# Graph network of three hops on one core: five chunks of ten groups, and four edits around them

## The reference

```python
agg = h; out = 0; rel = edge_emb[edge_type]
for _ in range(3):
    left  = agg[head] @ q_w
    right = tanh((rel * agg[tail]) @ k_w)
    att   = sum(left * right, axis=1)
    w     = softmax of att over the edges of one head
    summed = segment_sum(w[:, None] * rel * agg[tail], head)
    agg   = summed / max(cnt, 1)
    agg   = agg / max(norm(agg), 1e-12)
    out   = out + agg + h
return x + out
```

## Time and profile before

| | us |
|---|---|
| median of 3 runs (lowest, highest) | 2566.2 (2558.34, 2572.57) |
| the profiled execution | 2568.1 |
| its span | 2566.3 |
| PE busy (matmuls) | 1126.9, 44% |
| DVE busy | 1454.0, 57% |
| ACT busy | 858.7, 33% |
| POOL busy | 1190.2, 46% |

### The profile page before, as it was taken

One profiled execution on the slowest core, in us unless ns is written; L12 is line 12 of the kernel. 1 busy time (PEld: TensorE's weight loads), 2 busy tenths in 40 slices (PEclk: granted clock), 3 DMA queues, 4 the chain that ended last, 5 costly groups with the idle time before them and its releaser, 6 DMA issues. The chain is left out here.

```text
span 2566.3 us, 24723 instructions
## 1 busy us (share of the span) xinstructions
PE 1126.9 (44%) x5196; PEld 897.6 (35%) x5196; DVE 1454.0 (57%) x7228; ACT 858.7 (33%) x2657; POOL 1190.2 (46%) x1219
## 2 busy tenths in 40 slices
PE   0112333355454545553100257688734667655430
PEld 0011222244344324453100135467623455454320
DVE  8863664453364545544339657667654644657664
ACT  3312442332333423333126433344433232222320
POOL 1034434454545354466650255552035554647666
PEclk9999655555565655556555577788567777765555
DMA  5532322221222222322225464453144644636654
GB/s 203 207 139 88 129 93 67 68 80 57 71 67 68 71 71 70 115 80 92 77 81 213 172 189 146 132 150 109 63 153 139 189 127 115 174 85 168 168 142 130
DMA packets 192463, 305.35 MB, mean 119 GB/s; under 512 B 31210, under 2 KB 113458, under 8 KB 183686
## 3 DMA queue, kind: packets, MB, share of 16 engines
q1 hardware_dynamic: 153914, 230.79, 26.9%
q0 software_dynamic: 38400, 72.99, 10.8%
HBM read 176.41 MB, written 132.67 MB: 120 GB/s over the span
## 5 line engine op out<-in xcount | busy, mean ns | idle before, releaser
L646 POOL DMA_INDIRECT tr<-in_x_dram,tidx x200 | 191.4, 957 | 508.4 <-DMA acc_d<-xr 297.1
L1574 PE MATMUL ps<-rt,wr 128*125 128x128 f32 x1200 | 266.3, 392 | 245.1 <-issue 85.0
L1503 PE MATMUL ps<-ident,rt 128*128 128x128 f32 x600 | 144.6, 385 | 449.2 <-DVE rt L1169 206.8
L646 POOL DMA_INDIRECT tr<-agg_d,tidx x200 | 191.9, 959 | 288.4 <-DMA agg_d<-rt 138.4
L1574 PEld LDWEIGHTS ps<-rt,wr 128*125 128x125 f32 x1200 | 233.0, 288 | 263.4 <-DVE wr L1094 145.5
L1381 ACT ACTIVATE sqj<-ps,invc 125x128 bf16<-125x128 f32 x600 | 212.3, 373 | 328.5 <-remote 161.1
L646 POOL DMA_INDIRECT tr<-ntab_d,tidx x200 | 193.7, 969 | 260.9 <-DVE rt L1169 196.3
L1341 ACT COPY turns<-ps 128x512 f32<-128x512 f32 x150 | 87.8, 585 | 617.1 <-PE ps L1503 351.1
L1503 PEld LDWEIGHTS ps<-ident,rt 128*128 128x128 f32 x600 | 98.0, 196 | 482.0 <-issue 248.4
L1094 DVE TENSOR_SCALAR wr<-segbc,lcol,wcol 128x125 f32<-128x125 uint8 x600 | 177.9, 349 | 153.7 <-remote 111.4
L658 POOL DMA_INDIRECT ntab_d<-rt,lidx x200 | 202.1, 1011 | 134.2 <-DVE rt L1118 75.1
(11 more groups left out here) (239 smaller groups left out, 2456.2 us busy)
## 6 DMA issues: line engine op xcount, KB each, us to landing
agg_d<-rt SPq DMA_DIRECT2D x100, 258.0 KB
xr<-agg_d SPq DMA_DIRECT2D x100, 258.0 KB
relr<-rel_d SPq DMA_DIRECT2D x100, 256.0 KB
ntab_d<-rt SPq DMA_DIRECT2D x10, 2519.5 KB
acc_d<-xr SPq DMA_DIRECT2D x50, 258.0 KB
rel_d<-relr SPq DMA_DIRECT2D x50, 256.0 KB
hr<-acc_d SPq DMA_DIRECT2D x50, 256.0 KB
hr<-agg_d SPq DMA_DIRECT2D x50, 256.0 KB
```

Source lines behind the costliest of these rows:

```text
L646: G.indirect_dma_start(out=row, out_offset=None, in_=table[:, :], in_offset=bass.IndirectOffsetOnAxis(ap=idx[:, n:n + 1], axis=0)).then_in ...
L1503: ins = T.transpose(ps[B_TR][:, t, :], rt[:, g * GT + t, 0:D], ident[:, :])
L1574: ins = T.matmul(ps[B_T + j % 2][0:R, t, :], wr[:, (j % 2) * GT + t, 0:R], rt[:, j * GT + t, 0:D], start=True, stop=True)
```

## The change

Five edits.

1. **Chunks.** `K = 5`, chunks of ten groups each. Hop 0 has 25 units, all pairs. A chunk has 40 tiles where it had 52 (the last one 44); the arrays of the setup have five blocks instead of four, so their places in the scratch change. The negated flags are no longer kept for all chunks: `gneg` holds those of one chunk and is made in stage 0 behind its question. `PARTS` becomes `[40, 20, 20]`, `PLACES = [3, 3, 3]`: hops 1 and 2 get a third place at the end of a step, and ACT's `exp` stands behind its other work of the step. In hops 1 and 2 the sums of a chunk begin at steps 18, 28, 38 and 48; the loops hold the sums of 15, 34 and 17 groups, and 35, 16 and 33 are left.
2. **Dense blocks.** Seven early ones in hop 0's loop, three late ones in each of hops 1 and 2 (steps 1, 7, 13); the twelve between the hops stay.
3. **Norms.** `norms` takes the weights of the group as a list and puts one weight instruction behind each of its first steps; before, all four weights stood ahead of the norms and their wait for ACT. In the loops of hops 1 and 2 weights stand elsewhere, as before.
4. **Scaling put off.** `FILL = [5, 3, 5]`; between the stages of the last softmax stand only the weights of the `FILL` groups. Their scaling (and the norms that fall there) comes with the mixed sums, two groups of scaling a sum, until none is left. In hop 1 one mixed sum remains, so PE makes all parts of the last chunk ahead of one sum.
5. **The end of a hop.** The last norms are taken for three groups and then for two, each with its scaling behind it; in `scale` of hop 2 the two additions are one instruction a tile instead of one a group.

The diff, without the lines of the scratch's places:

```diff
@@ -23,8 +23,8 @@
-K = 4
-GC = [0, 13, 26, 39, NG]
+K = 5
+GC = [0, 10, 20, 30, 40, NG]
@@ -35,7 +35,7 @@
-NDE = 5
+NDE = 7
@@ -50,7 +50,7 @@
-LATE_AT = [1, 7, 13, 19]
+LATE_AT = [1, 7, 13]
@@ -72,10 +72,10 @@
-PLACES = [3, 2, 2]
+PLACES = [3, 3, 3]
 ...
-PARTS = [26, 13, 13]
+PARTS = [40, 20, 20]
@@ -124,7 +124,7 @@
-FILL, HOLD = 5, 2
+FILL, HOLD = [5, 3, 5], 2
@@ -132,7 +132,7 @@
-    return sums_left(h)[FILL:len(sums_left(h)) - HOLD]
+    return sums_left(h)[FILL[h]:len(sums_left(h)) - HOLD]
@@ -141,7 +141,7 @@
-    return sums_left(h)[i:i + 1] if i < FILL else range(0)
+    return sums_left(h)[i:i + 1] if i < FILL[h] else range(0)
@@ -211,10 +211,9 @@
         onesr = sb("onesr", [1, P])
-        gf = sb("gf", [Q, K, R], BF16)
-        gb = sb("gb", [Q, K, R], BF16)
-        gfn = sb("gfn", [Q, K, R], BF16)
-        gbn = sb("gbn", [Q, K, R], BF16)
+        gfb = sb("gfb", [Q, 2, K, R], BF16)
+        gf, gb = gfb[:, 0, :, :], gfb[:, 1, :, :]
+        gneg = sb("gneg", [Q, 2, R], BF16)
         gcol = sb("gcol", [Q, 2, K])
@@ -917,8 +916,6 @@
-            ch.note(V.tensor_scalar(gfn[:, :, :], gf[:, :, :], BIG, -BIG, ALU.mult, ALU.add))
-            ch(V.tensor_scalar(gbn[:, :, :], gb[:, :, :], BIG, -BIG, ALU.mult, ALU.add))
@@ -945,10 +942,10 @@
                 n, part = CT[b], slice(TC[b], TC[b + 1])
-                marks = (gf, gb) if add else (gfn, gbn)
+                marks = (gf[0:n, b, :], gb[0:n, b, :]) if add else (gneg[0:n, 0, :], gneg[0:n, 1, :])
                 lines = (G_, GN, WGF, WGB) if add else (GNEG, GNNEG, WGFN, WGBN)
                 return (n, (ALU.mult, ALU.add) if add else (ALU.add, ALU.max), 0.0 if add else LOWEST,
-                        [m[0:n, b, :] for m in marks], [rows[:, k, part] for k in lines])
+                        marks, [rows[:, k, part] for k in lines])
@@ -1015,6 +1012,7 @@
                     ask()
+                    ch.note(V.tensor_scalar(gneg[0:n, :, :], gfb[0:n, :, b, :], BIG, -BIG, ALU.mult, ALU.add))
                 elif stage == 1:
@@ -1097,18 +1095,30 @@
-            def norms(h, i):
-
-                dve.wait_ge(s_nr, h * NG + NB * (i + 1))
-                v, y, a, z = (nwt[0:R, k, :] for k in range(4))
-                ch(V.tensor_scalar(v, ssq[0:R, i % 2, :], 1e-30, None, ALU.max))
-                ch(V.tensor_scalar(y.bitcast(I32), v.bitcast(I32), -0.5, RSQRT_BITS, ALU.mult, ALU.add))
+            def norms(h, some, between=()):
+
+                between = list(between)
+
+                def step(ins):
+                    ch.note(ins)
+                    done = ch.at
+                    if between:
+                        between.pop(0)()
+                    dve.wait_ge(s_dve, done)
+                dve.wait_ge(s_nr, h * NG + some[-1] + 1)
+                u = some[0] // NB
+                here = slice((some[0] - u * NB) * GT, (some[-1] + 1 - u * NB) * GT)
+                v, y, a, z = (nwt[0:R, k, here] for k in range(4))
+                step(V.tensor_scalar(v, ssq[0:R, u % 2, here], 1e-30, None, ALU.max))
+                step(V.tensor_scalar(y.bitcast(I32), v.bitcast(I32), -0.5, RSQRT_BITS, ALU.mult, ALU.add))
                 for k in range(3):
-                    ch(V.scalar_tensor_tensor(a, y, -0.5, y, ALU.mult, ALU.mult))
-                    ch(V.tensor_tensor(a, a, v, ALU.mult))
-                    ch(V.scalar_tensor_tensor(z, a, 1.5, y, ALU.add, ALU.mult))
+                    step(V.scalar_tensor_tensor(a, y, -0.5, y, ALU.mult, ALU.mult))
+                    step(V.tensor_tensor(a, a, v, ALU.mult))
+                    step(V.scalar_tensor_tensor(z, a, 1.5, y, ALU.add, ALU.mult))
                     y, z = z, y
-                ch(V.scalar_tensor_tensor(nsc[0:R, :], y, 1e12, invc[0:R, i * NB * GT:(i + 1) * NB * GT], ALU.min, ALU.mult))
+                step(V.scalar_tensor_tensor(nsc[0:R, here], y, 1e12, invc[0:R, some[0] * GT:(some[-1] + 1) * GT], ALU.min, ALU.mult))
+                for work in between:
+                    work()
@@ -1124,19 +1134,26 @@
                 ch.join()
-                ch(V.tensor_tensor(edge_rows(j)[0:R], edge_rows(j)[0:R], one_in[j % 2][0:R], ALU.add))
-                V.tensor_tensor(edge_rows(j)[0:R], edge_rows(j)[0:R], two_in[j % 2][0:R], ALU.add).then_inc(s_ag, 1)
-
-            def scaled(h, j):
+                for t in range(GT):
+                    n = j * GT + t
+                    ch.note(V.tensor_tensor(rt[0:R, n, 0:D], rt[0:R, n, 0:D], one_in[j % 2][0:R, t, :], ALU.add))
+                ch.join()
+                for t in range(GT):
+                    n = j * GT + t
+                    ins = V.tensor_tensor(rt[0:R, n, 0:D], rt[0:R, n, 0:D], two_in[j % 2][0:R, t, :], ALU.add)
+                ins.then_inc(s_ag, 1)
+
+            def scaled(h, j, between=()):
+                if j >= LAG and (j - LAG) % NB == 0:
+                    norms(h, range(j - LAG, j - LAG + NB), between)
+                else:
+                    for work in between:
+                        work()
                 if j >= LAG:
-                    if (j - LAG) % NB == 0:
-                        norms(h, (j - LAG) // NB)
                     scale(h, j - LAG)
             def sums(h, j):
-                for work in weights(h, j):
-                    work()
-                scaled(h, j)
+                scaled(h, j, weights(h, j))
@@ -1277,21 +1294,33 @@
                             scaled(h, j)
+                    if h > 0:
+                        softmax(h, *stage_at(h, s, 2))
                     if h == 0 and s in COUNTS_AT:
 ...
                     for j in sum_behind(h, i):
-                        sums(h, j)
+                        for work in weights(h, j):
+                            work()
+                put_off = list(sums_left(h)[:FILL[h]])
                 for j in sums_mixed(h):
-                    sums(h, j)
+                    for work in weights(h, j):
+                        work()
+                    put_off.append(j)
+                    for k in put_off[:2]:
+                        scaled(h, k)
+                    put_off = put_off[2:]
+                for k in put_off:
+                    scaled(h, k)
                 carries(h, LAST)
 ...
                 scale(h, NG - LAG)
-                norms(h, NG // NB - 1)
-                for j in range(NG - NB, NG):
-                    scale(h, j)
+                for some in (range(NG - NB, NG - 2), range(NG - 2, NG)):
+                    norms(h, some)
+                    for j in some:
+                        scale(h, j)
                 if h == 0:
@@ -1410,14 +1439,14 @@
                             turned(h, s)
-                        if stage_at(h, s, 0)[1] == 3:
-                            exps(h, stage_at(h, s, 0)[0])
                         if 1 <= s <= NG:
 ...
                             dense(c, range(DC // 2, DC))
+                        if stage_at(h, s, 2)[1] == 3:
+                            exps(h, stage_at(h, s, 2)[0])
                     for j in sums_at(h, s - 1):
@@ -1601,6 +1630,7 @@
                         softmax(*stage_at(h, s, 1))
+                        softmax(*stage_at(h, s, 2))
                     parts(h, *parts_at(h, s))
```

4 lines of the change are left out of this document (2 added, 2 removed).

## The result

The changed kernel is slower: median 2701.0 us (2686.2 to 2720.0, 4 runs) against 2569.4 us (2558.3 to 2574.1, 4 runs) of the kernel before, a ratio of 1.052 with a 95% interval of 1.044 to 1.061. Its profiled execution has a span of 2707.6 us against 2566.3. The forecast was 2554.

The account below looks back on a forecast made before the run. No engine was full in the long stages, so waits between engines, chiefly around POOL's rows of issues, were taken as the bound. Terms -7 +1 -14 +0 +9 -16 +13 +0 sum to -14: 2568 to 2554 us, range 2498 to 2618.

Parts of the forecast that it names:

- Hop 1 and hop 2 loops: Both loops: fewer late blocks against more sums, one more chunk and a third place; +9 and +13 us.
- The third place: Hops 1 and 2 loops: eight bare answers of PE, the rest hidden; +2 us, bounds -4 and +16.
- -5 +6 +6: Hop 1 loop: one late dense block less -5, six more sums half hidden +6, one more chunk +6.
- -5 +6 +5 +5: Hop 2 loop: late block -5, chunk +6, three more sums +5, longer first row of POOL issues +5.
- rival of a flooded POOL: Hop 2: first row of issues costs +16, dry softmax not made good, additions +16; 2597 us, chance 0.21.
- Hop 1 tail: No POOL issues: shorter last softmax -6, fewer parts -2, sums -6, one group less -2; -16 us.
- The term of -24 for two rounds fewer: Hop 0 loop: 25 rounds instead of 27, each costing 12 us of POOL's waiting; bounds 0 and -33.
- The extra chunk: Hop 0 loop: one more chunk's questions to PE cost one wait; +10 us, bounds 0 and +30.
- The rival of regular rounds: Hop 0: without odd one-group rounds all run at 17.4 us a group; about 2625 us, chance 0.13.
- Hop 0 tail and dense blocks: Between hops 0 and 1: one group less -6, scaling put off from the last softmax -8; -14 us.
- Hop 2 behind the loop: Three groups fewer for POOL -15.6, POOL dry in the last softmax +15, additions by tile covered; sum 0.
- The rule of the stand-stills: After some 12 us of POOL issues without a gap, what waits for PE stands still until the row ends.

Follow-up runs that it names:

- all_pairs: The kernel before, four chunks, with hop 0 in 25 pairs of groups that may cross chunk borders instead of 27 units; ratio 1.005.
- four_off_hop1: four_chunks with the scaling put off in hop 1 alone; 1965.8 us, ratio 0.999 to the kernel before.
- four_chunks: The changed kernel with four chunks, the places, parts and dense blocks of the kernel before, and a fill of five in all hops; ratio 1.004.

## Why the prediction was wrong, step by step

**Hop 1 and hop 2 loops (+9 and +13 forecast, +50 and +63 measured, +32 and +51 on the later chips).** Two steps failed. The third place was priced at +2 with +16 as its worst, from the bare answer of 0.87 us and on the ground that DVE is busy 64% of the stage. And the doubled parts had no price at all: I counted parts only in the tail. Taken back together they bring 27 and 36 us in the changed kernel; put into the kernel before they cost 35 and 36 to 46. The reason given, "DVE is busy", was the wrong kind: it says how much work there is, not what stands ahead of an answer or idles for a question. For the parts it was PE's queue (parts, sum, turn, keys, back) that DVE's answer came behind. For the third place the mechanism was named rightly, that PE waits there for DVE, and its size was wrong: the one wait of stage 6 is 12.5 to 15.9 us a loop, and the place costs 17 us a loop with ten tiles, 28 in hop 2 with twenty, where +2 stood in the sum. The other terms of these loops hold in hop 1 within the noise: with the schedule taken back, what is left is +5, where -5 +6 +6 makes +7. In hop 2 it is +6 to +16 where -5 +6 +5 +5 makes +11, on chips without the stand-still that the last +5 was for. On the first chip that term was too small: ACT's wait rose by 26 us, and the idle time between PE's small matmuls in that loop from 18 to 36 us (gaps of over 0.5 us, counted from the timeline), about the +16 that stood as its worst and in the rival of a flooded POOL. The +63 of the first chip against +51 may lie there; that is read from the trace and not tested.

**Hop 1 tail (-16 forecast).** -16.0 us on the first chip, -16.0 on chip 8: the one stage without POOL issues, counted instruction by instruction. Its last softmax went from 23.0 to 15.4 us, -7.6 for -6.

**Hop 0 loop (-7 forecast; +28 and +13).** The term of -24 for two rounds fewer is contradicted on the first chip, where POOL's wait for the store went up by 28 us; on the later ones it has nothing to act on, since POOL waits 8.8 us for the store in all. The extra chunk was +10 and measures about +14 where there are no stand-stills. The early blocks cost nothing for +7. The rival of regular rounds had the right sign on the first chip; whether it is the cause of the 15 us by which that chip loses more can't be said, since all_pairs ran on a quiet one. Another candidate is in the trace: hop 0 makes all 40 tiles of parts in one step (26 before), and PE's gaps between those small matmuls in this loop rose from 44 to 73 us.

**Hop 0 tail and dense blocks (-14; +10 and -4).** The last softmax there fell from 38.2 to 17.7 us as put off, and the tail as a whole is 15 us longer: the work came back later, beside POOL's scatters, where engines stand still. This is read from the trace and not tested on that chip.

**Hop 2 behind the loop (0; +8 and -9).** The mechanism is as told: the last softmax took 17.8 us, POOL was busy 2.9 of them (22.6 of 31.7 before), and three groups fewer were left. four_off_hop1 and four_chunks show the put-off scaling as POOL's idle time. Additions by tile at 0: borne out. They neither cost nor gain a measurable time.

**Weights between the steps of norms (0), last norms in two parts (0).** The second is borne out: 90.5 us for 91 in hop 1's tail. The first was not run alone.

**The rule of the stand-stills** was right in the trace and treated as a property of the kernel. It is one of a chip or its state. It also said only that engines that wait for PE stand still, while PE's own parts stand still as well. It carried the hop 0 terms and two of the rivals. The loss itself didn't hang on it, since the ratio is 1.03 on the chips without it. The slow rivals (2597 and 2625) named other mechanisms, and the range ended at 2618, short of 2701. The forecast's own range of 2540 to 2570 isn't what its recipe gives: half of the distance to each bound, added up, is some 48 us down and 87 up, 2506 to 2641; the terms themselves said that slower was more open than faster. The rival of regular rounds adds up to 2629, and the chances of faster to 0.45.

Left open: why in hop 1 the third place costs nothing more once the parts are doubled, while in hop 2 the two add up to more than their sum; where the other 18 us of hop 1's loop on the first chip come from (its parts have no gaps there), and whether the gaps of parts make the other 12 in hop 2; what makes the stand-stills.

## What to carry to other kernels

When steps of a serial chain are packed closer, price each answer by what stands ahead of it in the queue of the engine that answers, parts and sums included, and not by the answer alone or by the asking engine's busy share. And where two questions follow with nothing between them on the answering engine, it idles until the second is asked: 3 to 4 us a chunk here. Spreading a block of small matmuls over more steps was worth more than starting its consumers earlier: ten tiles a step instead of twenty came two steps later and won 10 to 18 us a loop with three places, 28 and 8 with two. Work taken off a chain isn't a gain if it comes back where another engine needs it next: with scaling put off, hop 2's last softmax was 14 us shorter and POOL stood idle for it.

## What the runs showed of the hardware

The same kernel takes 2569 us in the first runs and 1965 to 1971 us on the five later chips, at granted clocks of 0.652 and 0.697 in the two profiled executions; the difference sits where POOL issues long rows of indirect DMAs (hop 0 loop 822 against 542 us, its tail 225 against 119), while the tail of hop 1, without any, takes 91 on both. In those first runs PE issued matmuls that waited for nothing in the profile 1.2 to 3.3 us apart while POOL issued its row; the idle time of this kind among the parts is 63.6 and 110.1 us in the two kernels there and 0.0 in both on chip 8.

The Trainium skill says in "SBUF — State Buffer", Who interferes with whom, that a DVE instruction with both inputs in SBUF contends with a GpSimd instruction that reads SBUF, through a shared port pair that it calls an exclusive lock. The scatters' 1.049 to 1.060 us beside additions of 0.69 us and 1.016 to 1.019 beside additions of 0.29 agree; that the ports are the cause is not shown, and the time of the whole did not move.
